# Transformer block on one core: three reorderings inside the loop over batch rows

## The reference

```
xn  = (x - mean(x)) / sqrt(var(x) + 1e-5)            # per token
qkv = xn @ w_qkv.T + b_qkv                           # 16 heads of 32
att = softmax(causal(q @ k.T / sqrt(32))) @ v
ffn = (silu((xn @ gate.T) * gate_s) * ((xn @ up.T) * up_s)) @ down.T * down_s   # 1408 wide
out = x + (att @ w_out.T + b_out) + ffn
```

## Time and profile before

| | us |
|---|---|
| median of 3 runs | 1941.37 (1941.12 to 1942.3) |
| the profiled execution | 1944.31 |
| its span | 1942.6 |
| PE busy | 1898.3 (98%) |
| DVE, ACT, POOL busy | 1333.2, 1294.1, 1376.0 |
| matmuls of the 14 mid periods | one period takes about 116.7 |

### The profile page before, as it was taken

The page is one execution under the profiler, slowest core; times in us unless marked ns, Lnnn a source line. Parts: engine busy times, 40 slices in busy tenths (PEclk is TensorE's granted clock), DMA queues, the critical chain, the costliest instruction groups (busy, mean ns, idle before and its releaser), DMA issues.

```text
span 1942.6 us, 48936 instructions
## 1 busy us (share of the span) xinstructions
PE 1898.3 (98%) x15875; PEld 919.1 (47%) x15875; DVE 1333.2 (69%) x3912; ACT 1294.1 (67%) x2315; POOL 1376.0 (71%) x1105
## 2 busy tenths in 40 slices
PE   5999999999999999999999999999999999999998
PEld 2444444444444444444444444444444444444443
DVE  8886766767666676766767666676766767667664
ACT  4876676666666676676766666676666766666574
POOL 1596687866678676687866778676687866778665
PEclk9999999999999999999999999999999999999999
DMA  9259777686876859777686876859678695876766
GB/s 341 47 93 161 145 121 150 116 152 130 151 144 110 160 104 162 137 122 150 115 153 129 152 145 109 158 103 166 135 122 148 114 156 126 150 147 112 132 131 120
DMA packets 840163, 267.93 MB, mean 138 GB/s; under 512 B 812976, under 2 KB 812976, under 8 KB 839344
## 3 DMA queue, kind: packets, MB, share of 16 engines
q1 hardware_dynamic: 839984, 265.15, 72.3%
HBM read 46.94 MB, written 16.78 MB: 33 GB/s over the span
## 4 chain that ended last, share of the span: by engine, by line
PE 72%; POOL 9%; issue 5%; DVE 5%; DMA 4%; SPq 3%; ACT 1%; DVEq 0%; POOLq 0%; ACTq 0%
PE ps L601 72%; POOL phl L1381 3%; POOL region_b L1338 3%; DMA p_t<-phl 3%; SPq L507 2%; DMA memory<-down 1%; POOL memory L1376 1%; DVE p L1268 1%; DVE memory L1059 1%; POOL rstd L1334 1%; SPq L587 1%; SPq L589 0%; DVE hidden_tmp L1201 0%; POOL region_a L1343 0%; POOL o_hl L1386 0%
## 5 line engine op out<-in xcount | busy, mean ns | idle before, releaser
L601 PE MATMUL ps<-x_t,memory 128*128 128x512 f16 x4376 | 994.8, 379 | 5.2 <-DVE qk L1151 2.0
L1381 POOL TENSOR_TENSOR phl<-p,phl 128x1024 f16<-128x1024 f32 x320 | 683.0, 2134 | 381.6 <-ACT phl L987 381.4
L977 ACT ACTIVATE p<-p,nmax 128x384 f32<-128x384 f32 (+3 forms) x1024 | 529.7, 557 | 275.9 <-DVE nmax L1268 256.7
L601 PEld LDWEIGHTS ps<-x_t,memory 128*128 128x128 f16 x4376 | 405.0, 97 | 494.0 <-issue 36.1
L1268 DVE CUSTOM_DVE_ANT_0 p<-ps,causal,cst 128x384 f32<-128x384 f32 (+3 forms) x1024 | 515.0, 546 | 98.2 <-PE ps L601 78.1
L987 ACT CAST phl<-p 128x1024 f16<-128x1024 f32 x320 | 334.1, 1044 | 40.1 <-DMA p_t<-phl 24.2
L601 PE MATMUL ps<-memory 128*128 128x512 f16 (+1 forms) x1705 | 340.5, 352 | 1.1 <-DVE bout_bc L1133 0.8
L1376 POOL TENSOR_TENSOR memory<-hidden_tmp,memory 128x512 f16<-128x512 f32 x176 | 205.0, 1165 | 70.4 <-ACT memory L949 70.4
L1276 DVE TENSOR_REDUCE ps<-ps 128x132 f32<-128x264 f32 (+1 forms) x320 | 122.0, 381 | 164.4 <-PE ps L601 164.3
L601 PEld LDWEIGHTS ps<-vv,p_t 128*128 128x128 f16 x5120 | 186.2, 96 | 92.6 <-issue 14.4
L601 PEld LDWEIGHTS ps<-memory 128*128 128x128 f16 (+1 forms) x1705 | 142.9, 100 | 159.6 <-issue 7.9
(11 more groups left out here) (81 smaller groups left out, 1319.1 us busy)
## 6 DMA issues: line engine op xcount, KB each, us to landing
region_b<-x SPq DMA_DIRECT2D x31, 1024.0 KB, 5.9
out<-region_b SPq DMA_DIRECT2D x64, 256.0 KB, 2.4
p_t<-phl SPq DMA_TRANSPOSE x640, 3.2
memory<-w_qkv SPq DMA_DIRECT2D x3, 1024.0 KB, 7.9
memory<-down SPq DMA_DIRECT2D x1, 2816.0 KB, 21.9
memory<-gate SPq DMA_DIRECT2D x1, 2560.0 KB, 9.5
memory<-up SPq DMA_DIRECT2D x1, 2560.0 KB, 15.3
region_a<-o_hl SPq DMA_TRANSPOSE x66, 3.3
```

The source lines that it names most:

```text
L601: return nc.tensor.matmul(o, lhsT=l, rhs=r, start=start, stop=stop, skip_group_check=True)
L977: last = nc.scalar.activation(cols, cols, ACT.Exp, scale=-1.0, bias=nmax[:, s % 2, i:i + 1])
L1381: g.tensor_tensor(phl[:, s % 2, 1, :], p32[:, s % 2, :], phl[:, s % 2, 0, :], ALU.subtract)\
```

## The change

Three edits, all for the mid periods (the ACT table is used by the last period too):

1. ACT, slot 13: k3's high half is taken ahead of the tanh of gate tile 9.
2. POOL, slot 12: the low half of chunk 12's probabilities is taken ahead of the normalising of token tiles 2 and 3.
3. SP: the four turns of the next row's input leave the head of slot 15 and stand between the turns of chunk 15's high half and low half.

```
@@ ACT_MID
-    "| | q3 u8 | x0 |", "g9 k3 | x1 | | |", ...
+    "| | q3 u8 | x0 |", "k3 g9 | x1 | | |", ...
@@ POOL_MID
-    "u5 | |", "u6 R0 n0 n1 | | u7", "n2 n3 | |", "u8 l0 | |", ...
+    "u5 | |", "u6 R0 n0 n1 | | u7", "| n2 n3 |", "u8 l0 | |", ...
@@ SP, ahead of the slot's own turns
-                    if s == (15 if prev else 13) and nxt:
+                    if s == 13 and not prev:
                         sp.wait_ge(sem["up_ready"], at(b, "up_ready", NT)).then_inc(wait_over["sp"], 1)
                         turn_x(b + 1)
@@ SP, the slot's own turns
                         sp.wait_ge(sem["p_hi"], at(b, "p_hi", s + 1)).then_inc(wait_over["sp"], 1)
                         sp.dma_start_transpose(p_t[:, i, 0, :, :], phl[:, i, 0, :]).then_inc(sem[name], 16)
+                        if s == 15 and prev and nxt:
+                            sp.wait_ge(sem["up_ready"], at(b, "up_ready", NT)).then_inc(wait_over["sp"], 1)
+                            turn_x(b + 1)
                         sp.wait_ge(sem["p_lo"], at(b, "p_lo", s + 1)).then_inc(wait_over["sp"], 1)
                         sp.dma_start_transpose(p_t[:, i, 1, :, :], phl[:, i, 1, :]).then_inc(sem[name], 16)
```

More of the change, by code:

```diff
@@ L184 @@
     "| | b0 b1", "| | b2 b3", "| | f0 f1", "| | f2 f3", "u0 | |", "| |", "| | u1", "u2 | |", "u3 | |", "| | u4",
-    "u5 | |", "u6 R0 n0 n1 | | u7", "n2 n3 | |", "u8 l0 | |", "u9 | u10 l1 |", "l2 l3 | |", "| |", "| |", "| |",
+    "u5 | |", "u6 R0 n0 n1 | | u7", "| n2 n3 |", "u8 l0 | |", "u9 | u10 l1 |", "l2 l3 | |", "| |", "| |", "| |",
     "| |",
```

## The result

| | before | after |
|---|---|---|
| median of the runs, us | 1941.38 (4 runs, 1941.12 to 1942.3) | 1957.97 (4 runs, 1957.13 to 1958.86) |
| the profiled execution, us | 1944.31 | 1958.37 |
| its span, us | 1942.6 | 1956.6 |

The changed kernel is slower: ratio 1.0085, 95% interval 1.0067 to 1.0102. The medians are 16.6 us apart, the spans of the two profiled executions 14.0: the profiled execution of before lies 2.9 us above its median, that of the changed kernel 0.4.

A forecast was written before the change was run, and what follows sets the result against it. PE's pace bounds the kernel; 26.0 us of new waits ahead of `r0` less 6.2 and 2.0 us gained make 17.9 us net, taking the median from 1941.4 to about 1959 us, range 1947 to 1966.

The forecast's parts named there:

- What bounds the kernel: Whole loop: goes at PE's pace, PE busy in all but 44 of 1942.6 us, no other engine above 71%.
- The SP edit: Slots 14 to 15: input turns issued later, so PE waits 1.86 us ahead of `r0` in each of 14 periods.
- E: The time at which PE ends the values of chunk 13; the forecast counts SP's turns and `r0` from it.
- the hold at issue: Among the four input turns on SP: one is held while the instruction queue moves 16 KB; 0.73 us taken.
- The bounds: PE's wait ahead of `r0`: 1.3 us with the smallest hold, 1.1 with none, 2.2 with the longest.
- the first rival: Ahead of `r0`: input comes in time, only the three edits' 8.2 us of gains remain, 1933 us; chance 5%.
- Chunk 15: Chunk 15's values, behind `r0`: old stall gone but covered by the new wait; low half seen at E + 11.50.
- The ACT and POOL edits: At `g10` and chunk 12: ACT gains 2.0 us, POOL removes what chunk 12 costs, nothing late comes of it.
- The sum: Whole kernel: 26.0 us lost, 6.2 and 2.0 gained, 17.9 net; median from 1941.4 to about 1959 us.
- the two did not cancel: Second rival: a new wait of about 0.6 us per period cancels the 8.2 us gain, 1941 us; chance 5%.
- The hold at issue was there in all 14 periods: Third rival, SP's input turns: no hold, wait 1.13 us per period, 1949 us; chance 17%.
- The fourth rival: PE's idle stretches: granted clock falls each time as well, 24 us more, 1983 us; chance 4%.

The follow-up runs named there:

- the kernel with the lowest median: Kernel before with the first input turn moved between chunk 14's two turns on SP, plus the ACT edit: 1937.4 us, ratio 0.9978.

## Why the prediction was right, and where it was lucky

The prediction was 1959 and slower with a chance of 89%; measured 1958.0. Point by point:

**What bounds the kernel.** Right: PE's pace, and the differences between the eleven kernels lie, within 2 us, in the few waits of PE at three places.

**The SP edit.** The mechanism and each term, against the same period: SP follows PE by 0.23 us (973.64 − 973.41: 0.23). First input turn at E + 1.80 (975.21 − 973.41: 1.80). From its issue to the last one's, 4.29 + 0.73 = 5.02 forecast, 4.86 measured. Landing 3.4 forecast, 3.33 measured. From landing to PE 0.14 forecast, 0.05 measured. PE ready at E + 8.50, forecast and measured. So the wait is 1.53 here and 1.56 on average, not 1.86. The mis-sized term is above all the hold at issue (0.73 forecast, 0.57 here, 0.61 on average), then the time from landing to PE, which I had taken from `p_t`, where the row and that of the earlier trace rows gave 0.13, and the landing itself (0.07). The bounds were not added up right: 1.3 and 2.2 us of wait give 1951 and 1964, not 1953 and 1966. Nor were spacing and landing steady over the 14 periods, as the first rival's case has it: in before the last turn took 3.34 to 4.25 us to land, and it landed 0.9 us in time on average, not half a us.

**Chunk 15.** Right: covered by the new wait, `r0` follows late and the values at once.

**The ACT and POOL edits.** Right in the changed kernel, where the two waits are gone; wrong as gains of their own. "Behind them on POOL the order is unchanged and the total is the same ... Nothing late comes of it" was the step that failed. The total is not the same: chunk 12's low half now waits 0.16 us for ACT, and chunk 14's comes 0.2 us later. Above all it compared POOL with POOL. What counts is POOL against PE: when PE stops less and POOL does not get earlier, the turn that hangs on POOL is later for PE. In the whole change this did not show, since the SP edit ties the train to PE instead. I had the sum right for the changed kernel and would have called the two edits without it 4.6 us faster; they are 6.9 us slower.

**The sum.** 14 × 1.86 − 8.2 = 17.9 was forecast for the profiled execution; measured by spans: 14.0, while the losses give 14 × 1.56, some 21.9, lost and 7.8 gained (2.6, 3.4 and 1.8). The median came out 1 us from the forecast because a second size was off the other way: the distance of the medians is 16.6, since before's profiled execution was slower than its median by 2.9 us, and the changed kernel's by 0.4. That part is luck. So the fair measure of my error is the 3.9 us by which the sum of the spans was over, not the 1 us of the medians.

**The rivals.** The input was not in time; the two did not cancel. The hold at issue was there in all 14 periods. The granted clock did not fall in the loop: over the stretch from 150 to 1800 us it is 1.00. (The page's clock row cannot tell: a slice is 49 us long and 9 means 90% or more, so that it shows a 9 in before even where 3.4 us at half the clock lie.) PE stood idle for at most 1.6 us there. The fourth rival set an idle stretch of 2.07 us, followed by no fall, against one of 2.87, followed by one. The other runs do not bear out that the length decides: at the same place of the first period 2.03 to 2.10 us were followed by 3.4 us at half the clock in four kernels, and 1.95 to 2.23 us by none in the other seven; in the last period 2.87 us (POOL edit) and 2.99 us (the kernel with the lowest median) were followed by none.

## What to carry to other kernels

Before a DMA is put ahead of others on a queue, write the queue down as a train: what starts it, how far apart the issues are, which consumer needs which car. Bringing one half of a pair forward gains nothing when the consumer needs both, and every car behind it is late by its length and its wait.

A wait that is removed upstream is a gain only if the next meeting point has slack against the engine that did not get faster, or if that engine waits for the faster one in between, as SP does for PE in the changed kernel. Measure the distance between the two engines' events there, not the length of each engine's own queue.

Look for a queue's idle time between two waits first: one turn moved into such a hole made the kernel 3.2 us faster, and took back the 16 us that the three reorderings had cost.

## What the runs showed of the hardware

A transposing DMA of 256 KB within SBUF is issued in 1.23 us, follows the one before it by 1.34 to 1.5, and lands 3.0 to 3.4 us after its issue when nothing disturbs it.

An instruction fetch of 16 KB on another queue, one packet of 0.9 to 1.7 us, disturbs such DMAs by far more than its share of the DMA time. The turn that was under way landed after 3.9 to 5.4 us instead of 3.4, depending on how far it had come, and one or both of the next two issues were held, by 0.1 to 1.5 us. The packets show what happens: mostly from 0.4 to 1.1 us after the fetch's start on, the turns' data all but stop on all 16 engines (8 to 15 GB/s in the changed kernel at 977.2 to 978.1 us), for 1.0 to 1.35 us in before, 0.7 to 1.15 in the changed kernel, 0.95 to 1.75 with the ACT and POOL edits. Then they move mostly at 240 to 290 GB/s, against some 200 in a train paced by its issues. At that pace a turn's 256 KB take 1.0 us, so the prediction's estimate of the data time fits, and the train is paced by its issues except around the fetch.

The fetch goes with PE: it starts 2.4 to 3.5 us after E in all 14 periods of all eleven kernels, while the first input turn is issued anywhere from E − 3.05 to E + 1.81. So moving the train by 0.55 us against PE changed which turn it hits. That the fetch causes the stop is argued from this coincidence in time; no run leaves the fetch out.

PE's idle stretches of 1.0 to 1.6 us, once per period, left the granted clock at full. After about 2 us it fell in four kernels out of eleven, after 2.8 to 3.0 us in nine.
